# The on-chip copies for layer 0's second weight layout move from SyncE's queue to ScalarE's, and w2's load behind block 1's rows

## The reference

```python
prev = x0 = r_inputs                       # (2048, 39, 16)
for i in range(3):
    Wr = Ws[i].reshape(h, M, 128)          # h = 39, 64, 64
    z = relu(einsum('bhk,bmk,hmf->bfk', prev, x0, Wr) + bs[i][None, :, None])
    results.append(z[:, :64])
    prev = z[:, 64:]
pooled = sum(concatenate(results, axis=1), axis=-1)
return pooled @ W_lin                      # (2048, 1)
```

## Time and profile before

| | us |
|---|---|
| median of 3 runs (2001.42 to 2001.85) | 2001.7 |
| the profiled execution's own time | 1997.76 |
| its span | 1995.8 |
| PE busy | 1987.0 |
| DVE busy | 1781.3 |
| ACT busy | 519.3 |

### The profile page before, as it was taken

One profiled execution on the slowest core, in us unless ns is written; L12 is line 12 of the kernel. 1 busy time (PEld: TensorE's weight loads), 2 busy tenths in 40 slices (PEclk: granted clock), 3 DMA queues, 4 the chain that ended last, 5 costly groups with the idle time before them and its releaser, 6 DMA issues.

```text
span 1995.8 us, 20316 instructions
## 1 busy us (share of the span) xinstructions
PE 1987.0 (100%) x6202; PEld 797.8 (40%) x6202; DVE 1781.3 (89%) x1166; ACT 519.3 (26%) x485; POOL 2.7 (0%) x8
## 2 busy tenths in 40 slices
PE   9999999999999999999999999999999999999999
PEld 3344433344333443334433344433344333443343
DVE  8988898888988889888899888898888988889888
ACT  1332133321233311333113332123321233311332
POOL 0000000000000000000000000000000000000000
PEclk9999999999999999999999999999999999999999
DMA  7997876677866678767697666876668866679610
GB/s 170 202 196 161 181 162 147 145 151 166 176 146 144 151 154 186 156 132 155 141 195 157 135 154 142 186 171 134 152 142 172 178 144 146 144 159 188 148 40 0
DMA packets 98773, 304.87 MB, mean 153 GB/s; under 512 B 21682, under 2 KB 22961, under 8 KB 98756
## 3 DMA queue, kind: packets, MB, share of 16 engines
q1 hardware_dynamic: 98540, 304.51, 72.1%
q10 hardware_dynamic: 216, 0.15, 0.0%
HBM read 304.12 MB, written 0.01 MB: 152 GB/s over the span
## 4 chain that ended last, share of the span: by engine, by line
PE 94%; SPq 2%; DVE 2%; DMA 1%; issue 0%; DVEq 0%
PE acc L587 66%; PE acc L680 25%; DVE prod L403 2%; PE acc L581 1%; PE acc L627 1%; PE acc L689 1%; SPq L241 1%; DMA x_rot<-x 1%; DVE prod L409 0%; SPq L229 0%; SPq L250 0%; SPq L208 0%; SPq L235 0%; DVE x_rot L377 0%; SPq L217 0%
## 5 line engine op out<-in xcount | busy, mean ns | idle before, releaser
L403 DVE TENSOR_TENSOR prod<-prev,x_bc 128x2048 f32<-128x2048 f32 x512 | 1138.5, 2284 | 4.1 <-PE acc L587 4.0
L587 PE MATMUL acc<-prod,w_sb 128*128 128x512 f32 x2428 | 1050.7, 593 | 0.2 <-DVE prod L403 0.2
L587 PEld LDWEIGHTS acc<-prod,w_sb 128*128 128x128 f32 x2428 | 458.7, 190 | 590.8 <-issue 569.8
L680 PE MATMUL acc<-prod,w_sb 128*64 128x512 f32 x2432 | 530.9, 594 | 2.7 <-DVE prod L403 2.7
L756 ACT ACTIVATE prev<-acc,bias 64x1024 f32<-64x1024 f32 x126 | 139.8, 1109 | 1282.7 <-PE acc L587 1252.3
L587 PE MATMUL acc<-x_rot,w_new 128*128 128x512 f32 (+1 forms) x744 | 324.6, 592 | 0.0
L680 PEld LDWEIGHTS acc<-prod,w_sb 128*64 128x64 f32 x2432 | 170.9, 137 | 358.7 <-issue 300.1
L765 ACT ACTIVATE prev<-acc,bias 32x1024 f32<-32x1024 f32 x256 | 283.3, 1107 | 4.2 <-DVE prev L519 0.2
L409 DVE TENSOR_TENSOR prod<-prev,x_bc 128x1024 f32<-128x1024 f32 x191 | 227.7, 1219 | 1.5
L377 DVE TENSOR_TENSOR x_rot<-x_rot,x_rep 128x1024 f32<-128x1024 f32 (+1 forms) x188 | 216.7, 1220 | 5.6 <-DMA x_rot<-x 5.6
L587 PEld LDWEIGHTS acc<-x_rot,w_new 128*128 128x128 f32 (+1 forms) x744 | 141.1, 190 | 178.6 <-issue 177.8
(11 more groups left out here) (52 smaller groups left out, 107.5 us busy)
## 6 DMA issues: line engine op xcount, KB each, us to landing
x_bc<-x SPq DMA_DIRECT2D x312, 256.0 KB, 14.7
x_bc<-x SPq DMA_DIRECT2D x156, 512.0 KB, 20.6
x_rot<-x SPq DMA_DIRECT2D x155, 312.0 KB
x_rot<-x SPq DMA_DIRECT2D x223, 156.0 KB
x_bc<-x SPq DMA_DIRECT2D x124, 128.0 KB, 10.7
x_rep<-x SPq DMA_DIRECT2D x62, 192.0 KB
x_rot<-x SPq DMA_DIRECT2D x124, 44.0 KB
x_rep<-x SPq DMA_DIRECT2D x31, 128.0 KB
```

Of the source, the lines that this page charges most:

```text
L403: mul = nc.vector.tensor_tensor(prod[:, s:s + w, :], twice, x_bc[:, u, t:t + w, :], ALU.mult)
L587: mm = nc.tensor.matmul(acc[:, h, :], w, rhs[:, BANK * h:BANK * h + BANK], start=start, stop=stop)
L680: mm = nc.tensor.matmul(acc2[HALF * h:HALF * h + HALF, u, :], w2_sb[:, ORDER[pos], :], prod[:, pos % RING, BANK * h:BANK * h + BANK], star ...
```

## The change

`load_w0_new` is moved from SP's program to ScalarE's, and called behind `evacuate0_first()`. The copies, their order and the semaphores that they wait for and count are the same. On SP the load of `w2` is issued behind `load_pairs(1)`, ahead of block 1's x_bc. TensorE's, VectorE's and GpSimd's programs stay as they are. In the changed file the same lines have other numbers: L208 to L235 are the same, L267 is L240, L280 is L253, L288 is L261, L318 is L294, L241 and L250 are L770 and L779; TensorE's lines are 28 lower (L587 is L559), ScalarE's L756, L765, L772 and L785 are L728, L737, L744 and L757.

```diff
--- before.py
+++ after.py
@@ -234,33 +234,6 @@
                 for p, n, c, first in rest:
                     sp.dma_start(x_rot[p:p + n, c, :], x[i, first:first + n, :]).then_inc(rot_loaded[g], 16)
 
-            def load_w0_new():
-
-                def put(p, n, c, q, of, step=1):
-                    stop = q + (n - 1) * step + 1
-                    sp.dma_start(w0_new[p:p + n, c, :], w0_sb[q:stop:step, of, :]).then_inc(w0_new_loaded, 16)
-
-                def at(i, d):
-                    return 2 * (i - IC) + d - (D - 2)
-
-                top = DPC * M
-                sp.wait_ge(w0_new_cleared, 1)
-                sp.wait_ge(w0_ready, 1 + len(W0_REST))
-                for c0, c1 in ((0, MIXED), (MIXED + 1, C0)):
-                    sp.dma_start(w0_new[0:top, c0:c1, :], w0_sb[0:top, c0:c1, :]).then_inc(w0_new_loaded, 16)
-                put(0, QUAD, MIXED, 0, MIXED)
-                put(QUAD, M - QUAD, MIXED, at(QUAD, D - 2), C0, 2)
-                put(M, top - M, MIXED, M, MIXED)
-                put(top + QUAD - M + MIXED_D, M - QUAD, MIXED, QUAD, MIXED)
-                for c in range(2):
-                    put(top, IC, c, top, c)
-                    put(top + IC, MORE - IC, c, at(IC, D - 2 + c), C0, 2)
-                put(top, MORE, 2, at(D, D - 1), C0, 2)
-                put(top, MORE, 4, at(D + 1, D - 2), C0, 2)
-                for q in range(P // QUAD):
-                    put(QUAD * q, BOTH - 1, C0, at(MORE, D - 2), C0)
-                    put(QUAD * q + BOTH, LEFT - BOTH, C0, at(QUAD - 1, D - 1), C0, 2)
-
             def load_pairs(i):
 
                 for r, n in ((0, 48), (48, 48), (96, P - 96)):
@@ -315,11 +288,10 @@
                 sp.dma_start(bias[HALF * g:HALF * g + HALF, 2:3], b2[0:HALF, :]).then_inc(small_loaded, 16)
                 sp.dma_start(wl_col[HALF * g:HALF * g + HALF, 1:2], w_lin[2 * HALF:3 * HALF, :]).then_inc(small_loaded, 16)
             sp.dma_start(wl_col[:, 0:1], w_lin[0:2 * HALF, :]).then_inc(small_loaded, 16)
-            sp.dma_start(w2_sb[:], w2).then_inc(w2_loaded, 16)
-            load_w0_new()
             sp.wait_ge(acc0_full, 1)
             load_left([1])
             load_pairs(1)
+            sp.dma_start(w2_sb[:], w2).then_inc(w2_loaded, 16)
             load_bc_t1(1, 1, bc_loaded[1][BC_T1])
             load_bc_groups(1, 1, range(SOON))
             sp.wait_ge(split_used, 2)
@@ -791,6 +763,33 @@
                 act.wait_ge(sum01_ready, 1)
                 keep01(acc0[:, 0, :, :], 0, 0)
 
+            def load_w0_new():
+
+                def put(p, n, c, q, of, step=1):
+                    stop = q + (n - 1) * step + 1
+                    act.dma_start(w0_new[p:p + n, c, :], w0_sb[q:stop:step, of, :]).then_inc(w0_new_loaded, 16)
+
+                def at(i, d):
+                    return 2 * (i - IC) + d - (D - 2)
+
+                top = DPC * M
+                act.wait_ge(w0_new_cleared, 1)
+                act.wait_ge(w0_ready, 1 + len(W0_REST))
+                for c0, c1 in ((0, MIXED), (MIXED + 1, C0)):
+                    act.dma_start(w0_new[0:top, c0:c1, :], w0_sb[0:top, c0:c1, :]).then_inc(w0_new_loaded, 16)
+                put(0, QUAD, MIXED, 0, MIXED)
+                put(QUAD, M - QUAD, MIXED, at(QUAD, D - 2), C0, 2)
+                put(M, top - M, MIXED, M, MIXED)
+                put(top + QUAD - M + MIXED_D, M - QUAD, MIXED, QUAD, MIXED)
+                for c in range(2):
+                    put(top, IC, c, top, c)
+                    put(top + IC, MORE - IC, c, at(IC, D - 2 + c), C0, 2)
+                put(top, MORE, 2, at(D, D - 1), C0, 2)
+                put(top, MORE, 4, at(D + 1, D - 2), C0, 2)
+                for q in range(P // QUAD):
+                    put(QUAD * q, BOTH - 1, C0, at(MORE, D - 2), C0)
+                    put(QUAD * q + BOTH, LEFT - BOTH, C0, at(QUAD - 1, D - 1), C0, 2)
+
             def evacuate1(i, a, used):
                 act.wait_ge(chunk_used, used + RING)
                 spread(prev[1], acc1, 1)
@@ -816,6 +815,7 @@
             act.sem_inc(res2_ready, 2)
             act.wait_ge(bias0_loaded, 16)
             evacuate0_first()
+            load_w0_new()
             act.wait_ge(small_loaded, 16 * SMALL)
             for i in range(U):
                 evacuate1(i, i, i * (2 * CH) + CH)
```

## The result

The changed kernel takes 2005.99 us (median of 13 runs, 2001.61 to 2007.69), the kernel before 2001.42 (median of 13, 1999.28 to 2003.25): a ratio of 1.0023, 95% interval 1.0016 to 1.0030. It is slower by 4.6 us. The forecast was 1999.4, a gain of 2.3; the time lies within the range given, but on the other side of no change. The profiled execution took 2006.46 us, with a span of 2004.4.

A forecast was written before the change was run, and what follows sets the result against it. PE, busy for 1987.0 of 1995.8 us, was taken to bound the kernel. The one term, -2.32 us in the first layer-2 pass, taken off the median of 2001.7 gave 1999.4 us, range 1998.4 to 2006.5.

The forecast's parts named there:

- SP's queue: SyncE's issuing: block 1's first load at about 23.1, 13.57 us sooner; w2 from about 39.
- rival C: SP's queue: ScalarE's issues slow SP's, so the rows land no sooner; 2001.7 us, chance 0.03 together with another rival.
- The rows in time: Block 1's x_rot rows land by 52.6, before DVE starts at 54.16; its 4.74 us of waits go.
- The size of that gain: First layer-2 pass on PE: 18.78 us falls to 16.46 once DVE is on time, -2.32 us.
- the 0.03 for a gain of over 4 us: Whole kernel: chance 0.03 of over 4 us gained, which would need nearly twice the 2.32 us term.
- the case without a stall: PE's wait before L627 costs nothing and the full gain comes: 1999.4 us, chance 0.54.
- ScalarE: ScalarE's queue: 20 issues from 29.2 to about 42.6, over 17 us to spare before 59.99; cost 0.
- The wait that decides: PE's wait for all 20 copies before L627 at 59.79: copies in by 52.9, latest 57.8; cost 0.
- the bias load's 10.3 us: ScalarE's queue: landing time of a load issued at 8.03 beside SP's loads, added to the copies' last issue.
- Rival A: PE's wait before L627: copies late by issue order, landing about 64; stall 4.1, net +1.8 us, 2003.5; chance 0.20 within 0.2%.
- The argument against turns: DMA queues: served by turns, the bias load's packets would have gone in one or two us; it landed at 18.33.
- The clock: PE from L627 through layer 0: a stand-still could halve the clock, at most 11.6 us.

The follow-up runs named there:

- e10: The kernel before, all loads kept on SP, with the copies issued behind block 1's rows and ahead of w2: 1995.77 us, ratio 0.9976.
- e1: The changed kernel with each of the four 19-row copies cut into 16 + 3 rows: 1996.11 us, ratio 0.9977.
- e8: The kernel before, unchanged, profiled a second time: 2001.05 us, span 1999.1.
- e6: The changed kernel with SP waiting for all 20 copies before it issues w2's load and block 1's x_bc: 1995.56 us, ratio 0.9975.
- e5: The changed kernel with only the first of the four 19-row copies cut into 16 + 3 rows: 2003.69 us, ratio 1.0012.
- e7: The kernel before with the four 19-row copies cut into 16 + 3, all staying on SP: 2004.19 us, ratio 1.0019.
- e3: The changed kernel with w2's load back ahead of block 1's rows, the copies staying on ScalarE: 2004.96 us, ratio 1.0018.
- e4: The changed kernel with 8 idle matmuls of 512 columns on TensorE right before its wait for the copies: 2003.74 us, ratio 1.0015.

## Why the prediction was wrong

- **SP's queue, right.** First row load forecast at 23.1, measured 23.22; w2 at 39, measured 41.44: from the first x_rep to w2 SP took 12.9 us instead of 10.5, beside ScalarE's issues. In e10, where ScalarE issues nothing, the issues for the same rows took 9.0 us (28.61 to 37.56). So rival C's toll is real, some 3.9 us, but it was without effect.
- **The rows in time, right.** Both waits of DVE gone; the pass is 16.46 us long, in one piece, also in e1, where no stall hides late products.
- **The size of that gain, mis-sized.** 2.32 us is what the one profiled execution lost. That it was 3.9 us faster than the median stood in the text; I took the term for a difference that holds in every execution, but it was this term that had been small in it (e8: 5.15). That was bad luck in the choice of execution, and the 3.9 us were the warning. e1 and e6 gained 4.8 and 5.2 us. So the 0.03 for a gain of over 4 us was far too little for the case without a stall.
- **ScalarE, right in what matters, wrong in detail.** The issues took 24.93 to 39.80, 0.74 us each, and began 4.3 us before the eviction that they stand behind: the issues did not wait for the activations ahead of them in the program. Cost 0, as forecast.
- **"The wait that decides": the step that failed.** I took the bias load's 10.3 us as the nearest row and added it to the last issue, 52.9. The copies were in at 67.0. That row was the nearest in its queue and its busy neighbour, but not in shape: it has 128 rows, where the copies that were late have 19. What counts, by theory T, is how many rows a copy puts on one DMA engine, times the neighbour's time for a row, 0.33 us: 76 x 0.33 = 25 us, and the four copies were issued between 34 and 39.8, so they would be in at some 60 to 65; they were in at 67. The shapes were known and the 0.33 us follows from 4 KB rows at 200 GB/s; I did not multiply them. That the 76 rows lie on one engine is inferred from the rates and from e1; e5, where 17 rows fewer gave 2.9 us and not 5.7, shows that the product is a guide and not exact.
- **Rival A, right in place, near in size, wrong in its reason.** A stall of 4.1 us was priced, 7.0 came. But not by order of issue: the copies were issued before w2 and x_bc and came in behind much of them (SP's queue moved 3.16 MB from 48 to 64), and e1 took the stall away with no byte moved. The argument against turns, that the bias load's packets would have gone in a microsecond or two, was too quick: turns, row by row, are what the traces show for the copies once the neighbour's queue is full. The bias load itself stays unexplained: its 128 rows, if spread over 16 engines, are 8 on each, some 3 us by such turns, and it took 10.3. The Trainium skill's rule (turns between the queues, packet by packet) thus holds for the copies, with a turn of about one row; the conclusion "served at once" that I drew from it does not follow for many rows on one engine.
- **The clock, priced as an end and left out of the sum for rival A.** At most 11.6 us was the bound, 3.67 the price. Net, by the typical execution e8: 7.00 + (15.23 - 11.66) - 5.15 - 0.13 for the start = 5.3 us, and the medians say 4.6.

## What to carry to other kernels

When small transfers move to a queue of their own beside a full one, count the rows that each puts on one DMA engine and multiply by the neighbour's time for one of its rows; cut a count that puts all rows on one engine (19 into 16 + 3, e1), or see to it that the neighbour's queue is empty meanwhile (e6). Before using a second issuer, try the order in the first: e10 has all of the gain without it. And where the profiled execution is off the median by as much as the term in question, take a second profile before pricing the term.

## What the runs showed of the hardware that I had not expected

- Two queues on the same DMA engines: 46 rows of 512 B against 47 rows of 4 KB and more on each engine in 16 us, and 49 packets in 4 us where the other queue had paused, for 15 where it had not.
- PE's granted clock fell to 0.50 in or right after waits of 3.11 us (e7), 4.15 (e5), 6.80 (e3) and 7.00 (the changed kernel), and did not fall where 7.13 us of idle matmuls left 0.98 of waiting (e4); the lower level cost 2.9 (e3) to 3.7 us.
- The kernel before varies from run to run (1998.42 to 2003.61 among 32). In the two executions of it that were profiled, 3.3 us apart, the DMA engines' pace differs in one stretch, 56 to 68 us: 157 to 179 GB/s in e8, 199 to 216 in the profile that the prediction was read from, and SP came to block 1's rows 0.54 us later in e8. That this pace explains the other executions too is not shown. The versions that take the rows off the path vary by 0.7 to 1.4 us.
